# Another order of the work inside steps 1 to 5 of a fused attention and expert kernel

## The chip, the cores and the metric

The kernel runs on one core of a Trainium2 chip. The metric is the device time of one execution in microseconds (us). Each engine of the core (TensorE, VectorE, ScalarE, GpSimd, SyncE, in the profile PE, DVE, ACT, POOL, SP) has its own program; an instruction waits on semaphores, and everything behind it on its engine waits with it.

## The reference

Input x has 8 sequences of 256 tokens of width 256, and a context of the same shape. The layer adds an attention and then a mixture of experts:

```
x = x + attention(layernorm(x), ctx, ctx)          # 16 heads of 16, keys j < i only (and j = 0 for i = 0)
    scores = (q Wq)(k Wk)^T / 4 ; probs = softmax ; out = (probs (ctx Wv + bv)) Wo + bo
x = x + experts(layernorm(x))                      # 8 experts, 2 per token, at most 512 rows each
    top_k(softmax(x wg), 2) -> relu(x w1 + b1) w2 + b2, weighted by the gates
```

## The kernel before, in words

The function `attention` (line 45) handles the 8 sequences in a software pipeline of steps s = -2 to 8, written out by hand for every engine as a function `step(s)`; `experts` (line 1344) follows and is not changed. In a step s three sequences are at work: sequence s + 2 is normalised and projected to queries and keys; of sequence s + 1 the largest score of each row is found (the "maxima"), and its values are projected; of sequence s the scores, exponentials, masks and products with the values are made; and sequence s - 1 gets its output projection, second norm and router. Steps 1 to 5 contain all of these parts. Steps 0, 6, 7 and 8 have orders of their own.

Products in 32 bits are made from a high part (rounded by ScalarE) and a low part (the difference, from VectorE or GpSimd), in three matmuls: `project` and `project_turned` (lines 1113 and 1102) make 12 matmuls of 256 columns each. For the scores, queries and keys are cut in three bf16 parts h, m and l; SyncE copies each part to rows of a stacked tile, six transfers for queries and six for keys (`stack`, line 252), and one matmul over 126 or 128 rows then gives the score.

On TensorE `a_scores` (line 986) makes the maxima's scores in 12 units of two or four heads, in two PSUM banks in turn, so that a unit waits until VectorE has reduced the one two before it (`maxima`, line 718). Unit 0 also waits for all stacking transfers of the step before (lines 991 and 992). `split_maxima` (line 770), `turn_maxima` (line 1091) and ScalarE's `copy_maxima` (line 574) put the negative maxima into two more rows of the stacked queries by a transfer, for which `b_scores` of the next step waits (line 1009). `b_scores` (line 1006) makes the scores of a group of four heads in three banks (there is one such buffer, so the next group waits for the exponentials), `exp` (line 504) on ScalarE the exponentials, `mask` (line 390) on GpSimd the mask in three instructions, and `values` (line 1023) on TensorE the product with the values, line 1035 and 1036. ScalarE's `values` (line 513) copies two groups out. `turn_values` (line 1040) transposes them, `normalise` (line 727) divides by the sums, `turn_attention`, `outputs`, `turn_x2` and `router` follow on TensorE (lines 1081, 1147, 1085, 1164), with `round_attention`, `normalise_x2` and `copy_x2` on ScalarE (lines 519, 547, 552), `add_output`, `logits` and `top_two` on VectorE (lines 746, 765, 705).

Two PSUM banks, `bank[0]` and `bank[1]` (line 67), are shared by all of the small products. bank[0] takes the projected values, the second turned values, the transposed x, the keys and the router's result; bank[1] the first turned values, the transposed attention, the output projection, the queries, the transposed x2 and the turned maxima. So the order of these on TensorE sets which copies each must wait for.

The norm of x is made in parts: `next_stats` (VectorE, line 754), `norm_powers` (GpSimd, line 378) and `norm_x` (ScalarE, line 498), the last three sequences ahead of step s. `add_value_bias` (VectorE, line 735) waits for the values' projection, and the second `turn_values` waits for it (line 1047). `prefetch` (line 474) loads 1 MB of expert weights from ScalarE's queue.

## Time and profile before

| | us |
|---|---|
| median of 3 runs | 436.12 |
| lowest and highest of them | 433.43, 436.37 |
| profiled execution, its time | 436.96 |
| its span, first to last instruction | 435.2 |
| granted TensorE clock, mean over the span | 0.94 |
| busy in the span: PE, PEld, DVE, ACT, POOL | 372.6, 315.6, 291.4, 189.1, 213.5 |

The profile is one execution. Times in rows are us from the span's start. A row of a timeline has the start, the length (ns elsewhere), the engine, the line in the code, the operation with its output and inputs, how many instructions are merged (x4), and in brackets how long the engine idled before and what released it. PE are matmuls and PEld the weight loads, which overlap them. The end of a matmul contains the time in which its result drains, so a run of matmuls is best read from start to start. A row of busy time by stretch has the stretch and its length, then the busy time of PE, PEld, DVE, ACT and POOL with their counts of instructions, the granted TensorE clock (1.00 is 2.4 GHz), and the DMA engines' share and GB/s. Names of tiles stand without their numbers; tiles that share memory may stand under the name of another, such as w_hi and w_lo for the stacked queries and keys.

### The profile page before, as it was taken

The numbers are of one execution on the slowest core, as the hardware profiler recorded it, in microseconds if no ns is written. First come the engines' busy times: TensorE is split into PE (matmuls) and PEld (weight loads), VectorE is DVE, ScalarE is ACT, GpSimd is POOL, SyncE is SP. The second block draws the span as 40 slices with busy tenths as digits, with TensorE's granted clock in tenths as the row PEclk, the third lists the DMA queues.
The fourth block names the chain that finished last, engine by engine and source line by source line (L and its number), as shares of the span: only waits on it lengthen the run. The fifth ranks groups of instructions, "written<-read, shape, count | busy, mean of one in ns | idle before, by whom it ended". The sixth has DMA issues, their size and how long they took to land. (4 is left out here: it accounts for less than half of the span.)

```text
span 435.2 us, 8185 instructions
## 1 busy us (share of the span) xinstructions
PE 372.6 (86%) x3030; PEld 315.6 (73%) x3030; DVE 291.4 (67%) x627; ACT 189.1 (43%) x258; POOL 213.5 (49%) x305
## 2 busy tenths in 40 slices
PE   3686899999999997877453999999999999999991
PEld 3555676767776776665341899999999998989891
DVE  6576776776767666763781467786777778677840
ACT  4423555565646453664210535354353626262310
POOL 7659867574848372423226303526180817250532
PEclk9989999999999999986655899999999999999998
DMA  8983716060605164132223603728090918230223
GB/s 205 247 231 82 208 32 189 27 196 26 193 5 138 60 182 123 50 101 78 81 50 81 259 0 107 199 75 229 12 274 21 269 28 244 60 51 9 30 32 36
DMA packets 38315, 49.15 MB, mean 113 GB/s; under 512 B 7138, under 2 KB 34180, under 8 KB 37252
## 3 DMA queue, kind: packets, MB, share of 16 engines
q1 hardware_dynamic: 29636, 34.93, 27.7%
q0 software_dynamic: 6144, 8.33, 10.2%
q10 hardware_dynamic: 2496, 5.38, 3.9%
q8 instruction: 24, 0.39, 0.4%
q14 instruction: 15, 0.12, 0.1%
HBM read 27.60 MB, written 8.41 MB: 83 GB/s over the span
## 5 line engine op out<-in xcount | busy, mean ns | idle before, releaser
L1490 POOL DMA_INDIRECT out_dram<-Y,scatter_idx x32 | 51.3, 1603 | 106.5 <-DVE Y L1646 91.0
L1533 ACT ACTIVATE hr<-ps,b_sb 128x512 f32<-128x512 f32 x64 | 43.2, 686 | 99.5 <-PE ps L1690 57.5
L724 DVE TENSOR_REDUCE nm<-ps 128x2 f32<-128x512 f32 (+1 forms) x96 | 61.5, 681 | 17.4 <-PE ps L1003 17.2
L1700 PE MATMUL ps<-w_hi,h_hi 128*128 128x256 f32 x224 | 63.2, 282 | 0.0
L1700 PE MATMUL ps<-w_lo,h_hi 128*128 128x256 f32 x224 | 62.9, 281 | 0.0
L1700 PE MATMUL ps<-w_hi,h_lo 128*128 128x256 f32 x224 | 62.8, 280 | 0.0
L511 ACT ACTIVATE PT<-ps 128x1536 f32<-128x1536 f32 x32 | 46.5, 1452 | 22.7 <-PE ps L1019 21.7
L1621 DVE CAST h_hi<-hr 128x512 fp32r<-128x512 f32 x60 | 27.2, 454 | 39.2 <-ACT hr L1533 36.2
L1690 PE MATMUL ps<-XT_hi,w_hi 128*128 128x512 f32 x128 | 51.3, 401 | 1.5 <-DVE XT_lo L1604 1.5
L1690 PE MATMUL ps<-XT_hi,w_lo 128*128 128x512 f32 x128 | 51.2, 400 | 0.0
L1690 PE MATMUL ps<-XT_lo,w_hi 128*128 128x512 f32 x128 | 51.1, 400 | 0.0
L1700 PEld LDWEIGHTS ps<-w_hi,h_hi 128*128 128x128 f32 x224 | 42.2, 188 | 1.6
L1700 PEld LDWEIGHTS ps<-w_hi,h_lo 128*128 128x128 f32 x224 | 42.2, 188 | 1.5
L1623 DVE TENSOR_TENSOR h_lo<-hr,h_hi 128x512 fp32r<-128x512 f32 x60 | 41.7, 695 | 2.1
L1700 PEld LDWEIGHTS ps<-w_lo,h_hi 128*128 128x128 f32 x224 | 42.2, 188 | 0.0
L1477 POOL DMA_INDIRECT Xg<-xn_rows,gather_idx x32 | 32.5, 1014 | 12.5 <-issue 9.4
L1003 PE MATMUL ps<-mask,identb 128*128 128x256 bf16 (+1 forms) x96 | 30.0, 313 | 0.0
L1690 PEld LDWEIGHTS ps<-XT_hi,w_hi 128*128 128x128 f32 x128 | 24.6, 192 | 5.6 <-issue 1.9
L1690 PEld LDWEIGHTS ps<-XT_lo,w_hi 128*128 128x128 f32 x128 | 24.6, 192 | 5.5
L1690 PEld LDWEIGHTS ps<-XT_hi,w_lo 128*128 128x128 f32 x128 | 24.7, 193 | 3.9
L1035 PE MATMUL ps<-PT,V 128*32 128x256 f32 x256 | 22.0, 406 | 3.9 <-POOL PT L396 3.9
L394 POOL TENSOR_SCALAR_AFFINE_SELECT PT<-PT 128x4 f32<-128x4 f32 x32 | 6.5, 204 | 36.7 <-ACT PT L511 36.5
(234 smaller groups left out, 888.2 us busy)
## 6 DMA issues: line engine op xcount, KB each, us to landing
raw<-in_L_ffn_w_dram SPq DMA_DIRECT2D x12, 1024.0 KB
raw<-in_L_ffn_w_dram ACTq DMA_DIRECT2D x4, 1024.0 KB
c_sb<-in_ctx_dram SPq DMA_DIRECT2D x8, 256.0 KB, 4.3
xn_rows<-x2n SPq DMA_DIRECT2D x8, 256.0 KB, 3.0
out_dram<-x_all SPq DMA_DIRECT2D x8, 256.0 KB, 2.8
x_all<-in_x_dram SPq DMA_DIRECT2D x1, 1280.0 KB, 6.5
w_lo<-k_h SPq DMA_DIRECT2D x9, 128.0 KB, 3.5
w_hi<-q_h SPq DMA_DIRECT2D x9, 128.0 KB, 2.5
```

Of the source, the lines that this page charges most:

```text
L394: pool.affine_select(p0[:, :, 0:1], p0[:, :, 0:1], [[0, HPG], [0, 1]], ALU.is_ge, 0.0, base=0, channel_multiplier=-1)
L511: act.activation(PT[g % 2][:, :], prob_score, ACT.Exp, scale=float(HD) ** -0.5).then_inc(exp_done, 1)
L724: dve.tensor_reduce(nm[:, tile, h:h + count], max_bank[u % 2].rearrange("p (h j) -> p h j", h=count), AX_X, ALU.max, negate=True).then_inc ...
L1003: pe.matmul(diag, identb[:, :], mask1[:, :, :] if tile else mask0[:, :, :], start=False, stop=True, skip_group_check=True).then_inc(a_done, 1)
L1035: pe.matmul(out, V[s % 2][:, 0, h, :], PT[g % 2][:, hh * S:(hh + 1) * S], start=True, stop=False)
L1477: pool.indirect_dma_start(Xg[q][:, j, :], None, xn_rows[:, :], bass.IndirectOffsetOnAxis(ap=gather_idx[:, ST * e + j:ST * e + j + 1], axis ...
L1490: pool.indirect_dma_start(out_rows[:, :], bass.IndirectOffsetOnAxis(ap=scatter_idx[:, ST * e + j:ST * e + j + 1], axis=0), Y[q][:, j, :], ...
L1533: act.activation(hr[c % 2][:, :], h_bank[c % 4], ACT.Relu, bias=b1_sb[q][:, c:c + 1]).then_inc(hr_ready, 1)
L1621: dve.tensor_copy(h_hi_of(e, c), hr[c % 2][:, :]).then_inc(hh_ready, 1)
L1623: dve.tensor_tensor(h_lo_of(e, c), hr[c % 2][:, :], h_hi_of(e, c).bitcast(F32), ALU.subtract).then_inc(hl_ready, 1)
L1690: last = pe.matmul(h_bank[c % 4], w[q][:, k, c, :], a[q][:, k, :], start=(n == 1), stop=(n == 6))
L1700: last = pe.matmul(y_bank[j // 2][:, (j % 2) * D:(j % 2 + 1) * D], a[c % 4][:, j * P:(j + 1) * P], w[q][:, c, :], start=(c == 0 and n == 0 ...
```

## The change

Steps 1 to 5 get an order of their own on each engine.

- TensorE: maxima unit 0 stands between the two turned values; units are issued singly or in pairs through `unit_scores`. Keys are projected ahead of scores 2, and before queries. The output projection follows scores 1. The router and the turned maxima stand between values 2 and values 3, the maxima no longer wait for the router's copy but for the copy of x2. The next values' projection waits for the router's copy.
- VectorE: the top two of the router of the step before and the statistics of sequence s + 3 stand first, ahead of the value bias; the router's result is copied at the end of the step (`copy_logits`).
- ScalarE: `norm_x` of sequence s + 2 stands first in step s (before: that of s + 3 late in step s). `copy_maxima` and the last copy of values stand at the head of the next step, maxima first; exp 0 is ahead of rounding attention and x. The weights' load of step 5 comes last in it.
- GpSimd: powers of the next norm and the bias first, then the context; keys and queries are split on either side of mask 2.
- SyncE: stacks keys before queries, except in step 0.

```diff
--- before.py
+++ after.py
@@ -283,7 +283,7 @@
                 if proj_part(s):
                     if s + 2 >= BUFS:
                         sp.wait_ge(b_done, GROUPS * s)
-                    for row in (stack_keys, stack_queries) if s < 0 else (stack_queries, stack_keys):
+                    for row in (stack_queries, stack_keys) if s == 0 else (stack_keys, stack_queries):
                         row(s, to)
                 if out_part(s):
                     sp.wait_ge(x2n_ready, 2 * s)
@@ -419,6 +419,19 @@
                     mask(0, 2)
                     mask(0, 3)
                     norm_powers(3)
+                    return
+                if 0 < s < B - 2:
+                    if s + 3 < B:
+                        norm_powers(s + 3)
+                    add_bias(s + 2)
+                    split_context(s)
+                    mask(s, 0)
+                    mask(s, 1)
+                    powers(s - 1, ln2_stats, mv2, ve2, rs2, ln2_pow)
+                    split_keys(s)
+                    mask(s, 2)
+                    split_queries(s)
+                    mask(s, 3)
                     return
                 if proj_part(s):
                     split_context(s)
@@ -606,6 +619,27 @@
                     if score_part(s):
                         values(s, 1)
                     prefetch(s - (B - 2) + 2)
+                elif 0 < s < B:
+                    norm_x(s + 2)
+                    if s > 1:
+                        copy_maxima(s - 1)
+                        values(s - 1, 1)
+                    round_context(s)
+                    exp(s, 0)
+                    round_attention(s)
+                    round_x(s)
+                    exp(s, 1)
+                    round_keys(s)
+                    exp(s, 2)
+                    round_queries(s)
+                    normalise_x2(s)
+                    values(s, 0)
+                    exp(s, 3)
+                    copy_x2(s)
+                    if s == B - 3:
+                        copy_maxima(s)
+                        values(s, 1)
+                        prefetch(1)
                 else:
                     if proj_part(s) and s > 0:
                         round_context(s)
@@ -639,16 +673,12 @@
                     if score_part(s):
                         values(s, 0)
                         exp(s, 3)
-                    if 0 < s and s + 3 < B:
-                        norm_x(s + 3)
                     if s == 0:
                         copy_maxima(s)
                     if score_part(s):
                         values(s, 1)
                     if max_part(s) and s > 0:
                         copy_maxima(s)
-                    if s == 0:
-                        norm_x(3)
 
             round_weights(1)
             round_context(-2)
@@ -716,7 +746,10 @@
                     dve.tensor_copy(expert_all[:, k, bass.ds(2 * n, 2)], idx8[:, :, k]).then_inc(top_used, 1)
 
             def maxima(s, pair):
-                for u in (2 * pair, 2 * pair + 1):
+                unit_maxima(s, 2 * pair, 2 * pair + 2)
+
+            def unit_maxima(s, lo, hi):
+                for u in range(lo, hi):
                     dve.wait_ge(a_done, UNITS * (s + 1) + u + 1)
                     if u == 0 and not first(s, 0):
                         dve.wait_ge(nm_ready, 2 * (s + 1))
@@ -762,9 +795,12 @@
                     dve.wait_ge(xn_ready, 2 * (s + 2))
                 norm_stats(x_all[:, bass.ds(2 * (s + 3), 2), :], st1[(s + 3) % 2], mv1[(s + 3) % 2], ln1_stats, s + 3)
 
-            def logits(s):
+            def copy_logits(s):
                 dve.wait_ge(rt_done, s)
                 dve.tensor_copy(lg[:, :, :], bank[0][:, 0:2 * EXPERTS].rearrange("p (t e) -> p t e", t=2)).then_inc(lg_ready, 1)
+
+            def logits(s):
+                copy_logits(s)
                 top_two(s - 1)
 
             def split_maxima(s):
@@ -907,6 +943,29 @@
                     early_slots(1, 0)
                     early_slots(1, 1)
                     logits(s)
+                elif 0 < s < B:
+                    if s > 1:
+                        top_two(s - 2)
+                    if s + 3 < B:
+                        next_stats(s)
+                    add_value_bias(s)
+                    normalise(s, 0)
+                    unit_maxima(s, 0, 1)
+                    normalise(s, 1)
+                    unit_maxima(s, 1, 3)
+                    split_attention(s)
+                    split_x(s)
+                    unit_maxima(s, 3, 4)
+                    add_output(s)
+                    unit_maxima(s, 4, 5)
+                    split_keys(s)
+                    unit_maxima(s, 5, 8)
+                    split_queries(s)
+                    unit_maxima(s, 8, 12)
+                    split_maxima(s)
+                    copy_logits(s)
+                    if s == B - 3:
+                        top_two(s - 1)
                 elif s == 0:
                     maxima(s, 0)
                     maxima(s, 1)
@@ -985,8 +1044,11 @@
         def _(pe):
             def a_scores(s, pair):
 
+                unit_scores(s, 2 * pair, 2 * pair + 2)
+
+            def unit_scores(s, lo, hi):
                 Q, K = Qs[(s + 1) % BUFS], Ks[(s + 1) % BUFS]
-                for u in (2 * pair, 2 * pair + 1):
+                for u in range(lo, hi):
                     if u == 0:
                         pe.wait_ge(q_stacked, 96 * (s + 2))
                         pe.wait_ge(k_stacked, 96 * (s + 2))
@@ -1045,7 +1107,7 @@
                         pe.wait_ge(nmT_ready, s + 1)
                 elif max_part(s):
                     pe.wait_ge(v_ready, s + 2)
-                elif not score_part(s):
+                else:
                     pe.wait_ge(lg_ready, s - 1)
                 for g in range(GROUPS):
                     last = pe.transpose(bank[1 - t][:, g * P:(g + 1) * P], OT[:, g, t * P:(t + 1) * P], ident[:, :])
@@ -1091,7 +1153,7 @@
             def turn_maxima(s):
                 pe.wait_ge(nm_ready, 2 * (s + 2))
                 if out_part(s):
-                    pe.wait_ge(lg_ready, s)
+                    pe.wait_ge(x2T_ready, s)
                 else:
                     pe.wait_ge(k_rest_ready, s + 3)
                 for t in range(2):
@@ -1133,6 +1195,8 @@
 
             def keys(s):
                 pe.wait_ge(cT_lo_ready, s + 3)
+                if s > 0:
+                    pe.wait_ge(xT_lo_ready, s + 3)
                 if first(s, -1):
                     pe.wait_ge(w_lo_ready, 1)
                 project_turned(key_bank(s), 1, cT_hi, cT_lo, k_done)
@@ -1142,6 +1206,8 @@
                     pe.wait_ge(w_lo_ready, 3)
                 if s == 0:
                     pe.wait_ge(q_rest_ready, 1)
+                if s > 1:
+                    pe.wait_ge(lg_ready, s - 1)
                 project(values_bank(s), 2, cT_hi, cT_lo, v_done)
 
             def outputs(s):
@@ -1272,6 +1338,33 @@
                         turn_maxima(s)
                     if score_part(s):
                         values(s, 3)
+                elif 0 < s < B:
+                    project_values(s)
+                    turn_values(s, 0)
+                    unit_scores(s, 0, 1)
+                    turn_values(s, 1)
+                    b_scores(s, 0)
+                    unit_scores(s, 1, 3)
+                    turn_attention(s)
+                    turn_x(s)
+                    unit_scores(s, 3, 5)
+                    b_scores(s, 1)
+                    outputs(s)
+                    values(s, 0)
+                    keys(s)
+                    b_scores(s, 2)
+                    unit_scores(s, 5, 7)
+                    queries(s)
+                    unit_scores(s, 7, 8)
+                    values(s, 1)
+                    unit_scores(s, 8, 10)
+                    b_scores(s, 3)
+                    turn_x2(s)
+                    unit_scores(s, 10, 12)
+                    values(s, 2)
+                    router(s)
+                    turn_maxima(s)
+                    values(s, 3)
                 else:
                     if max_part(s):
                         project_values(s)
```

## Rows read from the trace of the kernel before

**Rows 1.** Busy time by stretch: step 2, and steps 7 and 8 to the experts' first matmul.

```profile
97.50:120.00 22.50, 20.86 (x220) 16.70 (x219) 16.08 (x42) 12.73 (x18) 14.30 (x26) 1.00 0.38 107
...
186.00:239.00 53.00, 29.65 (x247) 22.01 (x248) 28.65 (x84) 16.15 (x23) 19.66 (x32) 0.63 0.28 80
```

**Rows 2.** TensorE's waits in steps 1 to 5: total us, times, longest.

```profile
PE ps L1035 <- POOL PT L396: 3.5, 6, 0.6
PE ps L1051 <- DVE V L741: 2.1, 6, 0.3
PE ps L1120 <- DVE aT_lo L694: 1.6, 5, 0.3
```

**Rows 3.** TensorE's timeline of step 2: start, length, line, operation, idle before.

```profile
97.48 0.38 PE L1120 MATMUL ps<-w_hi,cT_hi 128*128 128x256 f32 x1
...
99.00 0.60 PE L1051 MATMUL ps<-ident,OT 128*128 128x128 f32 x4
...
113.39 0.95 PE L1174 MATMUL ps<-wg_sb,x2T 128*128 128x8 f32 x8
114.28 0.66 PE L1035 MATMUL ps<-PT,V 128*32 128x256 f32 x8
...
115.09 0.61 PE L1016 MATMUL ps<-w_hi,w_lo 128*128 128x256 bf16 x4
...
115.76 0.39 PE L1000 MATMUL ps<-Ks,Qs 126*128 126x128 bf16 x4
...
116.20 0.38 PE L1000 MATMUL ps<-Ks,Qs 126*128 126x256 bf16 x2
...
117.44 0.39 PE L1000 MATMUL ps<-Ks,Qs 126*128 126x256 bf16 x2
...
117.78 0.39 PE L1000 MATMUL ps<-Ks,Qs 126*128 126x128 bf16 x4
...
119.02 0.66 PE L1035 MATMUL ps<-PT,V 128*32 128x256 f32 x8 [0.64 <-POOL PT L396]
...
119.98 0.39 PE L1120 MATMUL ps<-w_hi,cT_hi 128*128 128x256 f32 x1
```

**Rows 4.** VectorE's timeline of step 2: split maxima before it, bias, statistics, reductions.

```profile
97.02 0.19 DVE L777 TENSOR_TENSOR nm_s<-nm,nm_s 128x32 bf16<-128x32 f32 x1
99.20 0.69 DVE L741 TENSOR_TENSOR V<-ps,bv_bc 128x512 f32<-128x512 f32 x1 [1.99 <-PE ps L1120]
...
109.30 0.74 DVE L681 BATCH_NORM_STATS2 st<-x_all 128x6 f32<-128x256 f32 x2
110.15 0.25 DVE L684 BATCH_NORM_AGGREGATE mv<-st 128x2 f32<-128x6 f32 x2
...
111.71 2.57 DVE L724 TENSOR_REDUCE nm<-ps 128x2 f32<-128x512 f32 x4
```

**Rows 5.** ScalarE's timeline of step 2: the copy of x2 and exp 3.

```profile
111.70 0.60 ACT L489 ACTIVATE x2T<-ps 128x512 f32<-128x512 f32 x1 [0.63 <-PE ps L1058]
...
115.96 1.45 ACT L511 ACTIVATE PT<-ps 128x1536 f32<-128x1536 f32 x1
```

**Rows 6.** GpSimd's timeline of step 2: the last instruction of mask 3.

```profile
118.32 0.65 POOL L396 TENSOR_SCALAR_AFFINE_SELECT PT<-PT 128x512 f32<-128x512 f32 x1
```

**Rows 7.** SP's timeline, steps 2 and 3: three transfers of a high part.

```profile
113.16 1.85 SPq L257 DMA_DIRECT2D w_hi<-k_h  x3
...
135.35 3.25 SPq L257 DMA_DIRECT2D w_lo<-k_h  x3
```

**Rows 8.** Transfers of steps 1 to 5: count, KB each, median us from issue to landing.

```profile
Qs<-q_l SPq DMA_DIRECT2D x2, 128.0 KB, 5.1
...
w_lo<-q_l SPq DMA_DIRECT2D x1, 128.0 KB, 2.6
```

**Rows 9.** VectorE's timeline at the end of step 0: the split maxima.

```profile
50.57 0.53 DVE L777 TENSOR_TENSOR nm_s<-nm,nm_s 128x32 bf16<-128x32 f32 x1
```

**Rows 10.** TensorE's timeline in step 6: its first scores.

```profile
168.82 0.61 PE L1016 MATMUL ps<-w_hi,w_lo 128*128 128x256 bf16 x4 [0.81 <-DMA w_hi<-nmT]
```

## The prediction

> **What bounds the kernel now.** I read four views in this order: busy time by stage, TensorE's waits, TensorE's timeline of one step, and then the other engines beside it.
>
> The stages show where the change acts. Steps 1 to 5 take 22.5 us each (step 2 stands in the rows; the four others repeat it to 0.1 us), 112.5 us together. TensorE is busy 20.9 us of such a step, VectorE 16.1, GpSimd 14.3, ScalarE 12.7, and the granted clock is 1.00, the 2.4 GHz level [rows 1]. TensorE therefore leads these steps, and only its idle time can be gained: no matmul is removed. The experts behind them are not touched.
>
> TensorE's waits name three idle places that come back in nearly every step: 0.6 us for the mask of the fourth group of probabilities, 0.35 us for the biased values, 0.3 us for the low half of the attention output [rows 2]. The timeline shows them in step 2, which runs from 97.48 to 119.98 [rows 3]. A wait also empties the array (its pipeline has run dry when the wait ends), so I count differently: which start-to-start times does the array need for the work itself? From [rows 3]: a projection 1.52 (97.48 to 99.00), router 0.89, values of a group 0.81, scores of a group 0.67, a four-head maxima unit 0.44, a two-head unit 0.34, turned maxima and what ends before them 0.96 with the last values (119.02 to 119.98), so 0.2 alone. Four transposes I put at 0.45 (an estimate: x4 stand with 0.60 including the drain). The step has 4 projections (6.1), 5 sets of transposes (2.25), 4 scores (2.7), 4 values (3.2), 8 two-head and 4 four-head units (4.5), the router (0.9) and the turned maxima (0.2): 19.85 us. So 22.5 - 19.85 = 2.65 us of each step are gaps, 13.2 us in five steps. This is the most that an order can give there.
>
> **The change part by part.** I walk one new step; times are us after its first projection starts, durations those of before. VectorE takes the biased values 1.72 after the step's start for 0.69 us [rows 4]; exp starts 0.87 after its scores start (115.09 to 115.96), takes 1.45, and its mask ends 1.6 after the exp ends (117.41 to 118.97) [rows 3, 5, 6].
>
> *Start.* Values' projection 0 to 1.52, first turned values to 1.97, maxima unit 0 to 2.31. The second turned values need the bias, done at 2.41, and start at 2.47: the 0.5 us gap of before is 0.16, since unit 0 fills it. Then scores 0 (2.92 to 3.59) and units 1, 2 (to 4.37). VectorE does normalise, unit 0, normalise in about 2.0 us from 2.3, to 4.3, just before the attention's transposes (4.37 to 4.82); x's follow to 5.3, units 3, 4 to 5.98, scores 1 (exp 0 ended at 5.24) to 6.65. ScalarE now does exp 0 ahead of rounding attention and x, so the low half of the attention output is ready at about 6.5; the output projection needs it only at 6.65. That gap is gone, with 0.1 to spare.
>
> *Middle.* Outputs to 8.17, values 0 to 8.98, keys to 10.5, scores 2 to 11.17, units 5, 6 to 11.95, queries to 13.47, unit 7 to 13.8, values 1 to 14.6, units 8, 9 to 15.4, scores 3 to 16.07. Each maxima unit must wait until VectorE has reduced the one two before it. VectorE's reductions come each 0.64 us [rows 4]; in my walk units 4, 6, 9, 10 and 11 find theirs done 0.1 to 1 us earlier. No gap, little room. The next statistics (0.74 and 0.25 with a semaphore between, 1.1 us, [rows 4]) and the top two of the previous router (nine small instructions, an estimate of as much again) now stand at the head of the step, where VectorE idled 1.99 us for the projection [rows 4]. They end at about 1.65, bias due at 1.72: they cost nothing, and would cost what they are late.
>
> *End.* x2's transposes to 16.5, units 10, 11 to 17.3, values 2 to 18.1. Exp 3 runs 16.27 to 17.72, then the copy of x2 (0.60, [rows 5]) to 18.25: the router waits 0.15 us and runs to 19.15, turned maxima to 19.37. The mask of group 3 ends at 17.72 + 1.6 = 19.3, so the last values start at 19.37 with almost no wait, where they stood idle 0.64 us (0.8 with the drain). This is the largest gain: between the last scores and the last values lay 3.93 us, of which 2.8 were filled; now the chain exp and mask is covered by x2, two units, values 2, router and turned maxima. Values end at 20.1. The next projection waits for the router's copy (about 19.6): nothing.
>
> The sum is 19.85 + 0.16 + 0.15, so 20.15. Splitting the units makes two more switches between kinds of matmul; each such first matmul starts about 0.08 later than one in a run, so 0.15 more: 20.3. Five steps give 5 x (22.5 - 20.3) = 11.0 us.
>
> *Transfers.* This is the added risk. Unit 0 stood behind both sets of turned values, scores 0 and two sets of transposes and is now 2 us into the step, and it needs all twelve stacking transfers of the step before. Keys first: their high part is ready at 11.3, and SP issues three in 1.85, so one each 0.62 us [rows 7]. GpSimd's two parts of each take some 1.9 us (an estimate: one of its 512-element instructions takes 0.65, [rows 6], and the second part has two inputs, so I count three of them). With them the last key transfer is issued at 14.6; queries follow from 15.2, the last at 18.4, ready on GpSimd since 17.3. It lands 2.6 us later [rows 8] at 21.0, unit 0 of the next step is due at 20.3 + 1.97 = 22.3: 1.3 us to spare. Not counted.
>
> *Step 6.* Its first scores waited 0.81 us for the turned maxima's transfer [rows 10]. These maxima are now turned ahead of the last values, 0.8 us earlier, and copied ahead of the last output copy. Between 0 and 0.97 us are gained (its other waits stay); I take 0.2 to 0.5, say 0.3. The load of expert weights moves behind step 5's copies, and about 15 us lie before its use: nothing lost, and it no longer runs among the stacking transfers. GpSimd's reordering and SP's keys ahead of queries only serve this order and are priced in it.
>
> *A lock.* In step 0 the second half of the split maxima took 0.53 us beside GpSimd's mask [rows 9], against 0.19 at the end of step 1 [rows 4]; in the new steps it falls beside the mask of group 3. At 0.53 the maxima are ready at 19.1, before the router has ended: nothing. The Trainium skill, "SBUF — State Buffer", section "SBUF: two separate sides", says that VectorE with two SBUF inputs and GpSimd exclude each other for whole instructions. By it the split could stand behind the last mask instruction, 19.3 + 0.2 = 19.5, which would put 0.3 us on each step, 1.5 in all.
>
> **The sum.** The profiled execution took 436.96 us (span 435.2). 436.96 - 11.0 - 0.3 = 425.7. The median of the runs, 436.1, is 0.84 lower, so I forecast 424.9.
>
> **The rivals.**
>
> *The stacking comes late, and it gets slower.* Unit 0 stands ahead of everything but the projection and one set of transposes; while it waits, TensorE's queue stands, and with it the scores, exp and masks. For it: the first three issues have taken 3.25 instead of 1.85 us once [rows 7], and two last query transfers took a median of 5.1 us [rows 8]. Each us beyond 1.3 counts fully, five times. Both in every step (2.8 from keys' and queries' issues, 2.5 from the landing) would be 5.3 - 1.3 = 4.0 us per step against 2.2 gained: 424.9 + 20 = 445. It decides from 3.5 us of lateness. Against it: the 5.1 contains a landing beside the 1 MB load, which moves away, and 3.25 stood in one step of five. Slower: 0.05.
>
> *VectorE becomes the bound in part.* It is busy 16.1 us a step [rows 1], some 17 with its own semaphores, and 20.3 leave 3. It must now wait in its order for unit 7 and the router's end. If maxima come 1 us late once or twice, a step takes 21.3: 425.7 + 5 - 0.8 = 430. The small margins above speak for it; that I took its durations with their semaphores speaks against. 0.17.
>
> *Nothing moves.* The gaps return elsewhere in the step: 22.2 to 22.5, so 433 to 436. That would want a loop through two steps that keeps the period; I find the longest one, scores 3, exp, mask, last values, projection, bias, below 20.2. 0.06.
>
> **How the numbers follow.** Forecast 0.72, its own range 421.5 to 428: below, every gap vanishes (13.2 + 0.97, 422 after rounding); above, 0.5 us more a step. With VectorE's case the range is 421 to 431. The clock adds its own uncertainty: it averages 0.63 between step 6 and the experts [rows 1], and where it returns may move, as the earlier runs spread by 3 us. About 1% can be told from no change: faster than 431.8 holds in the forecast and most of VectorE's case, 0.87; within 1% 0.08; slower 0.05.
>
> **What would show it.** Steps 1 to 5 about 20.3 us long; the wait of the last values for the mask near 0; the bias wait at 0.1 to 0.2; a short router wait for x2's copy; no wait of unit 0 for a transfer; statistics ahead of the bias; steps 6 onward as long as before. I am wrong if TensorE stands before unit 0, if maxima units wait for VectorE by more than 1 us in a step, or if the part behind step 5 grows.

## The result, and the profile after

The changed kernel takes 421.35 us (median of 3 runs, 419.91 to 422.76) against 436.12 us: the ratio is 0.9707 (95% interval [0.9666, 0.9747], as in all brackets behind a ratio). That is 14.8 us gained where 11.2 were forecast (424.9). It is inside the range of 421 to 431, at its lower edge, and just below the 421.5 at which the forecast's own range ended. The profiled execution took 422.76 us with a span of 421.0, so in the spans 14.2 us are gone. This section reads where they went; from here on "step n" starts with its first projection, as in the prediction.

Busy time by stretch of the changed kernel: step 3 and step 6 (columns: the stretch, its length, busy us and instructions of TensorE, its weight loads, VectorE, ScalarE, GpSimd; granted clock; share of the DMA engines; GB/s).

```profile
93.85:114.12 20.27, 19.87 (x219) 16.92 (x218) 16.45 (x44) 12.53 (x17) 14.26 (x26) 1.00 0.44 123
155.35:175.38 20.03, 17.06 (x192) 13.44 (x191) 14.67 (x40) 11.71 (x14) 7.06 (x16) 1.00 0.37 120
```

Step 3 holds TensorE busy for 19.87 of 20.27 us, where step 2 before held it for 20.86 of 22.50 [rows 1]. VectorE's and GpSimd's sums hardly move. TensorE's sum is 1.0 us smaller though no matmul was removed; the end of a matmul contains the time in which its result drains, so I read this as fewer stops behind which it shows (argued, not shown by a run). The five steps take 20.46, 20.27, 20.27, 20.27 and 20.96 us, before they took 22.44 to 22.51.

TensorE's waits in steps 1 to 5 of the changed kernel, 53.12 to 155.35 (us in total, times, longest).

```profile
PE ps L1078 <- DMA w_lo<-nmT: 0.7, 1, 0.7
PE ps L1062 <- issue: 0.3, 1, 0.3
```

These two stand where the five steps before had 6.5 us in three kinds of wait. ([rows 2] reaches into the steps on either side: from 52.53 to 164.93 the mask has 3.2 in 5 times and the bias 1.7 in 5.) The waits for the mask, the bias and the low half of the attention output are gone in all five steps. The wait of 0.3 is unit 0's in step 1. The 0.7 for the transfer of the turned maxima is in step 5, which is the one long step.

TensorE's timeline of step 3, changed kernel (start, length, engine, line, operation).

```profile
93.85 0.39 PE L1182 MATMUL ps<-w_hi,cT_hi 128*128 128x256 f32 x1
...
95.37 0.60 PE L1113 MATMUL ps<-ident,OT 128*128 128x128 f32 x4
96.05 0.39 PE L1062 MATMUL ps<-Ks,Qs 126*128 126x256 bf16 x2
...
96.39 0.60 PE L1113 MATMUL ps<-ident,OT 128*128 128x128 f32 x4
...
99.80 0.60 PE L1078 MATMUL ps<-w_hi,w_lo 128*128 128x256 bf16 x4
...
100.43 0.37 PE L1182 MATMUL ps<-w_hi,aT_hi 128*128 128x256 f32 x1
...
109.24 0.60 PE L1078 MATMUL ps<-w_hi,w_lo 128*128 128x256 bf16 x4
...
111.21 0.66 PE L1097 MATMUL ps<-PT,V 128*32 128x256 f32 x8
...
112.09 1.06 PE L1240 MATMUL ps<-wg_sb,x2T 128*128 128x8 f32 x8
113.20 0.29 PE L1160 MATMUL ps<-identb,nm_s 128*32 128x128 bf16 x2
113.32 0.65 PE L1097 MATMUL ps<-PT,V 128*32 128x256 f32 x8
...
114.12 0.38 PE L1182 MATMUL ps<-w_hi,cT_hi 128*128 128x256 f32 x1
```

Taken from 93.85, unit 0 starts at 2.20, the second turned values at 2.54, scores 1 at 5.95, the output projection at 6.58, scores 3 at 15.39, values 2 at 17.36, the router at 18.24, the turned maxima at 19.35, the last values at 19.47. The prediction's walk had 1.97, 2.47, 5.98, 6.65, 15.4, 17.3, 18.25, 19.15 and 19.37. No time of the walk is off by more than 0.25 us.

VectorE around the seam of steps 3 and 4, changed kernel: statistics and bias at the head, then the split maxima and the router's copy at the end.

```profile
94.09 0.74 DVE L711 BATCH_NORM_STATS2 st<-x_all 128x6 f32<-128x256 f32 x2
94.94 0.25 DVE L714 BATCH_NORM_AGGREGATE mv<-st 128x2 f32<-128x6 f32 x2
95.57 0.69 DVE L774 TENSOR_TENSOR V<-ps,bv_bc 128x512 f32<-128x512 f32 x1 [0.38 <-PE ps L1182]
...
112.19 0.34 DVE L811 CAST nm_s<-nm 128x32 bf16<-128x32 f32 x1
112.57 0.57 DVE L813 TENSOR_TENSOR nm_s<-nm,nm_s 128x32 bf16<-128x32 f32 x1
113.19 0.17 DVE L800 COPY lg<-ps 128x16 f32<-128x16 f32 x1
```

GpSimd's timeline beside it, the last instruction of mask 3.

```profile
112.46 0.65 POOL L396 TENSOR_SCALAR_AFFINE_SELECT PT<-PT 128x512 f32<-128x512 f32 x1
```

The idle time ahead of the bias fell from 1.99 [rows 4] to 0.38: the statistics fill it and still end in time. At the end the second half of the split took 0.57 us beside GpSimd's mask; it ended at 113.14, the mask at 113.11. The turned maxima and the last values follow at 113.20 and 113.32. So mask, maxima and router (112.09 + 1.06) end within 0.05 us of each other, and a further gain at one of them would find the two others there.

**The part behind step 5.** The profiled pair divides as follows (before less changed, from the starts of the same operations): steps up to 1, -0.6; steps 1 to 5, 10.2; step 6 to step 7's first turned values, 1.0 (21.08 to 20.03); from there to step 8's first turned values, 2.75 (18.94 to 16.19); to the experts' first matmul, 0.1; experts, 0.7. Together 14.2. TensorE's timeline shows the 2.75, first in the kernel before, then in the changed one.

```profile
186.01 1.97 PE L1051 MATMUL ps<-ident,OT 128*128 128x128 f32 x8 [1.16 <-ACT OT L517]
...
200.87 1.87 PE L1174 MATMUL ps<-wg_sb,x2T 128*128 128x8 f32 x8 [0.19 <-ACT x2T L489]
204.95 1.97 PE L1051 MATMUL ps<-ident,OT 128*128 128x128 f32 x8 [0.75 <-ACT OT L517]
```

```profile
175.38 1.09 PE L1113 MATMUL ps<-ident,OT 128*128 128x128 f32 x8 [1.16 <-ACT OT L530]
...
188.88 1.06 PE L1240 MATMUL ps<-wg_sb,x2T 128*128 128x8 f32 x8 [0.84 <-ACT x2T L502]
191.57 1.97 PE L1113 MATMUL ps<-ident,OT 128*128 128x128 f32 x8 [0.74 <-ACT OT L530]
```

The instructions are the same, but before they met the 1.2 GHz level twice, at the step's start (1.97 against 1.09) and at its router (1.87 against 1.06); the changed kernel met it only from 190.9 on. The prediction had put 0.3 us on all that lies behind step 5.

### The profile page after: what moved, and what is told of

It is laid out like the page before. It is cut to its first block and busy times, and to the rows that moved or that the text cites. A ratio compares the mean times of both kernels' runs of the same rounds, so it can differ in the third digit from the quotient of the medians.

```text
span 421.0 us, 8170 instructions
## 1 busy us (share of the span) xinstructions
PE 364.5 (87%) x3010; PEld 314.1 (75%) x3030; DVE 293.9 (70%) x627; ACT 188.2 (45%) x258; POOL 215.9 (51%) x305
## 5 line engine op out<-in xcount | busy, mean ns | idle before, releaser
L757 DVE TENSOR_REDUCE nm<-ps 128x2 f32<-128x512 f32 (+1 forms) x96 | 62.4, 682 | 18.7 <-PE ps L1065 11.2
L1570 POOL DMA_INDIRECT Xg<-xn_rows,gather_idx x32 | 34.9, 1090 | 12.3 <-issue 9.3
L1065 PE MATMUL ps<-mask,identb 128*128 128x256 bf16 (+1 forms) x76 | 22.5, 296 | 0.0
L1097 PE MATMUL ps<-PT,V 128*32 128x256 f32 x256 | 21.1, 390 | 1.5 <-POOL PT L396 0.7
```

The lines of the kernel that those rows point to most:

```text
L757: dve.tensor_reduce(nm[:, tile, h:h + count], max_bank[u % 2].rearrange("p (h j) -> p h j", h=count), AX_X, ALU.max, negate=True).then_inc ...
L1065: pe.matmul(diag, identb[:, :], mask1[:, :, :] if tile else mask0[:, :, :], start=False, stop=True, skip_group_check=True).then_inc(a_done, 1)
L1097: pe.matmul(out, V[s % 2][:, 0, h, :], PT[g % 2][:, hh * S:(hh + 1) * S], start=True, stop=False)
L1570: pool.indirect_dma_start(Xg[q][:, j, :], None, xn_rows[:, :], bass.IndirectOffsetOnAxis(ap=gather_idx[:, ST * e + j:ST * e + j + 1], axis ...
```

## The experiments

Two questions were open. Which parts of the new order carry the 2.2 us of a step: one of them, or only all together? And is what was gained behind step 5 the order's or only the clock's?

**1. Both kernels again.** No edit.

> The kernel before once more. Both theories: steps 1 to 5 take 112.4 us. Theory A, chance: the clock's fall, which in the first profile stood over step 7's first turned values, can stand elsewhere here, and the part behind step 6's start (270.3 us) comes out between 267 and 272. Theory B, the order sets it: the fall stands at the same place, 270.3 within 0.5. The ratio to the runs beside it is 1.000 within 0.004 by both.

> The changed kernel once more, to see which part of its gain is fixed and which moves. Both theories: steps 1 to 5 again take 102.2 us together (20.3 each, step 5 up to 0.7 more), step 6 starts about 155.4. Theory A, chance: where the granted clock falls in steps 7 and 8 and where it returns in the experts moves from execution to execution by up to about 3 us, so the part behind step 6's start (265.6 us in the first profile) comes out anywhere between 264 and 269, and the time between 419.5 and 425. Theory B, the denser steps themselves keep the clock up into step 7: the clock is again at its high level over step 7's first turned values (1.09 us for 8 transposes, not 1.97), and the part behind step 6's start is 265.6 within 0.5.

Measured: before again 435.34 us, ratio 0.9988 [0.9942, 1.0034], steps of 22.47 to 22.61. Changed again 423.69 (420.78 to 427.02), ratio 0.9765 [0.9674, 0.9857], steps 20.97, 20.27, 20.35, 20.26, 20.72. TensorE's timeline of before again has step 7 like this:

```profile
186.82 1.09 PE L1051 MATMUL ps<-ident,OT 128*128 128x128 f32 x8 [1.16 <-ACT OT L517]
...
200.35 1.88 PE L1174 MATMUL ps<-wg_sb,x2T 128*128 128x8 f32 x8 [0.23 <-ACT x2T L489]
204.43 1.97 PE L1051 MATMUL ps<-ident,OT 128*128 128x128 f32 x8 [0.75 <-ACT OT L517]
```

The same kernel, the same work: 17.61 us instead of 18.94, with the fall at the step's start gone. Changed again took 17.34, having met a fall there. What the five steps gain repeats to 0.2 us; what step 7 gains does not (2.75, then 0.3). Theory B, as it was put, has failed: the fall did not keep its place in either kernel.

**2. The end of the step alone, on the order of before.** Router and turned maxima ahead of the last values, ScalarE's and VectorE's order to suit; and then the whole end, with x2's transposes late, as in the changed kernel.

```diff
# tail_alone, TensorE; scores 5 is the pair of units 10 and 11
-                    if out_part(s):
-                        router(s)
                     if score_part(s):
                         values(s, 1)
                         b_scores(s, 3)
...
                         a_scores(s, 5)
+                    if out_part(s):
+                        router(s)
+                    if out_part(s) and max_part(s):
+                        turn_maxima(s)
                     if score_part(s):
                         values(s, 3)
-                    if max_part(s):
+                    if max_part(s) and not out_part(s):
                         turn_maxima(s)
# tail_whole, in addition, the end as it then reads
+                        a_scores(s, 4)
+                    if score_part(s):
+                        b_scores(s, 3)
+                    if out_part(s):
+                        turn_x2(s)
+                    if max_part(s):
+                        a_scores(s, 5)
+                    if score_part(s):
+                        values(s, 2)
```

> The kernel before with only the tail changed: router and turned maxima ahead of the last values, the router's copy behind the split maxima, the maxima copied first. My theory: the 0.8 us gap before the last values is filled, and the turned maxima's transfer starts earlier, 0.9 to 1.1 us less a step, step length 21.4 to 21.6, 4.5 to 5.5 us in all and up to 0.9 in step 6: time 0.985 to 0.990 of the kernel before. Rival, that one part of this order gives nothing while the others bound the step: 0.995 to 1.000.

> The kernel before with the whole tail of the changed one in its steps: units 8 and 9, scores 3, x2's transposes, units 10 and 11, values 2, router, turned maxima, last values; the copy of x2 behind exp 3. Theory, after the run with the router alone moved (where the last reductions took the place of the mask): the gap closes only if the maxima's reductions too are covered, here by values 2 and router behind unit 11; step length 21.6 to 21.9, so 3 to 4.5 us over five steps, with 0.1 to 0.2 us left before the last values. Rival, the tail is worth nothing as long as the first half has its gaps: 22.3 to 22.5, and a new wait of 0.6 us appears in the tail.

Measured: 433.35 us (0.9942 [0.9899, 0.9986]), steps of 22.37 to 22.42; and 434.14 (0.9989 [0.9947, 1.0032]), steps of 22.45 to 22.51. The mask wait did go in both. TensorE's waits of steps 1 to 5 show what took its place, first for the end alone, then for the whole end. (The wait for the low half of the attention output stayed too, 1.6 in both.)

```profile
PE ps L1098 <- DVE nm_s L777: 2.9, 5, 0.6
PE ps L1051 <- DVE V L741: 1.6, 5, 0.3
```

```profile
PE ps L1000 <- DVE nm L724: 2.8, 5, 0.6
PE ps L1051 <- DVE V L741: 1.6, 5, 0.3
```

Five times 0.6 us for VectorE: for the split maxima in the one, for the reduction that frees a unit's bank in the other. VectorE's reductions were late by about as much as the mask, and showed once the wait for the mask no longer hid them. My theory fell here, and with it the reading of [rows 2] in which the mask wait's 0.64 us are there for whoever covers the mask.

**3. The end and the middle together.** To the whole end were added the next statistics at the head of VectorE's step, and units 4 and 5 with their reductions ahead of the keys' projection. GpSimd's order stayed.

```diff
# VectorE
+                    if s + 3 < B:
+                        next_stats(s)
                     if max_part(s):
                         add_value_bias(s)
...
                         split_queries(s)
-                    if s + 3 < B:
-                        next_stats(s)
+                    if max_part(s):
+                        maxima(s, 2)
                     if proj_part(s):
                         split_keys(s)
                     if max_part(s):
-                        maxima(s, 2)
                         maxima(s, 3)
```

> The kernel before with the changed tail and also room for VectorE in the middle: the next statistics stand first in the step, and units 4 and 5 and their reductions ahead of the keys. Theory, after the run with the tail alone, in which the wait for the mask vanished and unit 6 waited 0.56 us for a reduction instead: the gap in the tail and the gap in the middle are one budget of VectorE, and both close together; step length 21.5 to 21.9 (22.5 less about 0.7 to 0.9), 3 to 4.5 us in all, no wait of a unit over 0.3. Rival, the period is kept by the start of the step (bias, low half of attention): 22.3 to 22.5 whatever is done behind.

Measured: 434.13 us (0.9971 [0.9934, 1.0008]), steps 22.35, 23.61, 23.53, 23.50, 21.42. The waits for reductions went, and the mask wait came back. The timelines of ScalarE (first row) and GpSimd at the seam of steps 1 and 2, and below them TensorE's:

```profile
70.79 1.45 ACT L511 ACTIVATE PT<-ps 128x1536 f32<-128x1536 f32 x1 [0.97 <-PE ps L1020]
...
71.71 0.23 POOL L366 TENSOR_SCALAR ve<-mv 128x2 f32<-128x2 f32 x1
...
73.26 0.20 POOL L371 TENSOR_TENSOR rs<-ve,rs 128x2 f32<-128x2 f32 x1
73.40 0.21 POOL L394 TENSOR_SCALAR_AFFINE_SELECT PT<-PT 128x4 f32<-128x4 f32 x1
...
74.18 0.65 POOL L396 TENSOR_SCALAR_AFFINE_SELECT PT<-PT 128x512 f32<-128x512 f32 x1
```

```profile
74.89 0.66 PE L1036 MATMUL ps<-PT,V 128*32 128x256 f32 x8 [0.83 <-POOL PT L396]
...
76.33 0.41 PE L1121 MATMUL ps<-w_lo,cT_hi 128*128 128x256 f32 x1
...
78.46 1.64 PE L1052 MATMUL ps<-ident,OT 128*128 128x128 f32 x8
```

Exp 3 had ended at 72.24 (70.79 + 1.45), but GpSimd's order still had the powers of the next statistics (71.71 to 73.46) between mask 2 and mask 3, and the mask started at 73.40. So the new place of these powers, at the head of GpSimd's step, is a part of the change in its own right, which the prediction had not priced apart. Then, in steps 2 to 4, the granted clock fell to the 1.2 GHz level just behind this idle stretch: projection matmuls took 0.41 instead of 0.28 and two sets of transposes 1.64. Steps 2 to 4 are 1.2 us longer each than step 1, which had the same mask wait and no fall. Step 5 has no further sequence to norm, so no powers stand ahead of its mask 3; it had neither mask wait nor fall and took 21.42, where the kernel before took 22.47. So about 1.1 us of the 2.2 is there by then, read from one step of one profile. This run bears out neither theory whole.

**4. One part of the new order undone.** Each on the changed kernel: the router and the turned maxima behind the last values; unit 0 behind both sets of turned values and scores 0 (with its reduction); exp 0 behind the roundings of attention and x.

```diff
# router_last
                     values(s, 2)
+                    values(s, 3)
                     router(s)
                     turn_maxima(s)
-                    values(s, 3)
# unit0_behind
                     turn_values(s, 0)
-                    unit_scores(s, 0, 1)
                     turn_values(s, 1)
                     b_scores(s, 0)
-                    unit_scores(s, 1, 3)
+                    unit_scores(s, 0, 3)
# exp0_behind
-                    exp(s, 0)
                     round_attention(s)
                     round_x(s)
+                    exp(s, 0)
                     exp(s, 1)
```

> The changed kernel with router and turned maxima behind the last values in steps 1 to 5. My theory, that these two cover the chain exp, mask: the last values now wait for the mask 1.1 to 1.3 us, router and turned maxima (1.1) come after them, and the next projection waits 0.2 for the router's copy, so each step is 1.1 to 1.4 us longer: 5.5 to 7 us, 427 to 428.5. Rival, that the gain of these steps comes from their first half (bias, low half of attention) and the tail's order is hidden: under 2 us, below 423.5.

> The changed kernel with unit 0 behind both turned values, as before. Theory: the wait for the biased values is back, 0.35 us idle and 0.5 with the drain instead of 0.1: 0.3 to 0.4 us a step, 20.6 to 20.7, 1.5 to 2 us in all. Rival 1, VectorE has no room: units 1 and 2 are reduced 0.6 us later, and further waits of units follow, 20.9 or more. Rival 2: hidden by later room, 20.3.

> The changed kernel with exp 0 behind the rounding of attention and x on ScalarE. Theory: exp 0 starts 6.2 instead of 3.8 us into the step and ends 7.6, scores 1 start 1.6 us later, and with them everything behind: step length 21.6 to 22.0, 7 to 8.5 us more. Rival, the scores' buffer has room in this order: under 0.5 us a step.

| kernel | median us | ratio to before | steps 1 to 5 | over changed (102.2) |
|---|---|---|---|---|
| router last | 430.41 | 0.9884 [0.978, 0.9987] | 109.8 | 7.6 |
| unit 0 behind | 428.12 | 0.9875 [0.9794, 0.9955] | 106.9 | 4.7 |
| exp 0 behind | 428.49 | 0.986 [0.9779, 0.994] | 110.4 | 8.2 |

The long waits of each in TensorE's queue over steps 1 to 5, in the order of the table:

```profile
PE ps L1097 <- POOL PT L396: 5.4, 5, 1.1
```

```profile
PE ps L1061 <- DVE nm L757: 2.3, 5, 0.5
PE ps L1112 <- DVE V L774: 1.6, 5, 0.3
```

```profile
PE ps L1078 <- ACT PT L524: 7.1, 5, 1.4
```

Router last has one fall of the granted clock in it, in step 4 (mean 0.93, 22.68 us where its others take 21.59 to 21.87), so some 0.8 of its 7.6 us are the clock's; the other two have none. Each part taken out brings its own wait in every step: the mask (1.07 us in each), the bias and the reductions, or exp 0 itself, for which scores 1 now stood 1.4 us. Unit 0 is the telling one. The bias wait of 0.35 returns and costs what the prediction gave it, but 0.5 comes on top because VectorE, later by one reduction, holds a unit up further on: the rival that VectorE has no room was right where it was tested. Against them stands experiment 2: the end alone, put on the old order, is worth 0.1 us a step or nothing. (The start alone was not tried on it.) I read the 2.2 us as those of three chains (ScalarE's exps, GpSimd's masks, VectorE's reductions) that come due together; the waits that replace each other in experiments 2 to 4 show it for these parts, while the keys' new place and the halves of GpSimd's split were not undone by themselves.

**5. The transfers.** Queries stacked ahead of keys on the changed kernel, so that the last keys leave late; and two 64 KB transfers more on SP's queue between the keys' and the queries' in each of the five steps.

```diff
# queries_first
-                    for row in (stack_queries, stack_keys) if s == 0 else (stack_keys, stack_queries):
+                    for row in (stack_keys, stack_queries) if s < 0 else (stack_queries, stack_keys):
# extra_2
                         if row is stack_queries and 0 < s:
                             for _ in range(2):
                                 sp.dma_start(extra_rows[2 * (s - 1) + _], ident[:, :]).then_inc(extra_done, 16)
```

> The changed kernel with SyncE stacking queries ahead of keys in steps 1 to 5. Theory, that unit 0 stands 1.2 us behind the last landing: the last key transfer is now issued about 21.0 us into the step and lands 2.5 us later, unit 0 waits for a transfer in steps 2 to 5 (and the units of step 6 do not), step length 21.2 to 21.7, 4 to 6 us more in all. Rival, that the landing has more room than I read: no wait of unit 0, 20.3 us a step.

> The changed kernel with two more transfers of 64 KB issued by SyncE between the keys' and the queries' stacking in steps 1 to 5. In the changed kernel's trace the last query transfer lands 0.8, 0.05, 1.4 and 0.8 us before unit 0 of steps 2 to 5. The extra ones make it 1.2 to 1.3 us later. Theory, that this room is all there is: unit 0 waits 0.4, 1.2, 0 and 0.4, and the steps are longer by as much, 1.5 to 2.5 us in all. Rival, my forecast's room of 1.3: no wait.

Measured for queries first: 438.92 us (437.9 to 439.91), ratio 1.0118 [1.0036, 1.02], steps 20.82, 22.48, 24.10, 21.62, 21.79. For two more transfers: 426.76 (422.4 to 428.13), 0.9795 [0.9763, 0.9828], steps 20.18, 20.98, 20.79, 20.27, 21.31. TensorE's waits of steps 1 to 5 for queries first and, below, for the two transfers:

```profile
PE ps L1062 <- issue: 8.5, 5, 2.4
```

```profile
PE ps L1068 <- DMA w_hi<-q_l: 1.9, 2, 1.1
PE ps L1068 <- DMA Qs<-q_l: 0.7, 1, 0.7
```

SP's timeline of queries first at the start of step 3 (93.16):

```profile
91.36 1.83 SPq L257 DMA_DIRECT2D Ks<-k_h  x3
93.24 1.52 SPq L257 DMA_DIRECT2D Ks<-k_m  x2
94.81 0.61 SPq L257 DMA_DIRECT2D Ks<-k_l  x1
```

The last key transfer is issued 1.65 us into the step whose unit 0 needs it at 2.2. Keys are projected first, so behind the queries they wait for no reason, and all the rest of TensorE's queue waits with unit 0. The five steps take 110.8 us, 8.6 more than changed (one fall of the clock, in step 3, is in that), and the expectation of 4 to 6 was too small. It also said that step 6 would be spared, and there the longest wait stood:

```profile
169.38 0.58 PE L1062 MATMUL ps<-Ks,Qs 126*128 126x256 bf16 x2 [4.98 <-issue]
```

The last keys of step 5 were issued at 162.26, behind the 1 MB load (161.27), and took 7.0 us to land. Step 6 took 26.15 us instead of 20.03, again with a fall of the clock. So this is the rival of the late stacking: in the five steps it takes most of the gain away (110.8, before 112.4), and only step 6 makes the kernel slower than before, by 1.2% in the medians. The one line of the diff in SP's loop is what keeps it away. Two more transfers make three waits, 2.6 us together, of which 1.3 remain in the five steps (103.5 against 102.2): a delay of about 1.2 us (two issues of 0.61) is on the edge. In the changed kernel the last query transfer of steps 1 to 4 lands at 74.72, 96.0, 114.69 and 135.62, and unit 0 of the next step starts at 75.5, 96.05, 116.1 and 136.45. The forecast 1.3 us to spare were 0.8, 0.05, 1.4 and 0.8. The 0.05 is no margin at all but a short wait: the weight load of unit 0 in step 3 (PEld) stood idle for this transfer.

```profile
PEld ps L1062 <- DMA Qs<-q_l: 0.3, 1, 0.3
```

**6. The load of expert weights at its old place**, in the middle of step 5's work on ScalarE, all else as changed.

```diff
                     normalise_x2(s)
+                    if s == B - 3:
+                        prefetch(1)
                     values(s, 0)
                     exp(s, 3)
                     copy_x2(s)
                     if s == B - 3:
                         copy_maxima(s)
                         values(s, 1)
-                        prefetch(1)
```

> The changed kernel with step 5's 1 MB load back at its earlier place, ahead of the third copy of values. Theory: the load's packets stand among step 5's stacking transfers and delay the turned maxima's transfer, for which step 6's first scores wait again, 0.5 to 1 us, while step 5 itself stays at 20.7 to 21.0: 0.5 to 1.5 us in all. Rival 1: step 6's units wait for the stacked queries as well, more than 2 us. Rival 2: nothing, since the transfer of the maxima starts earlier in this order.

Measured: 426.13 us (423.75 to 430.41), ratio 0.9764 [0.9719, 0.9809]. The profiled execution took 430.41 us, so I compare step 6 alone. It starts at 155.42, in the changed kernel at 155.35. TensorE's timeline of its first scores, here and in the changed kernel:

```profile
161.40 0.65 PE L1079 MATMUL ps<-w_hi,w_lo 128*128 128x256 bf16 x4 [2.89 <-DMA w_hi<-nmT]
```

```profile
158.31 0.60 PE L1078 MATMUL ps<-w_hi,w_lo 128*128 128x256 bf16 x4
```

The 1 MB load was issued at 148.82, among the stacking transfers and 6.5 us ahead of the turned maxima's 16 KB on ScalarE's own queue. The transfers of q's high part took a median of 6.7 us to land (2.8 in the changed kernel), and the maxima's landed 6 us after its issue at 155.28. Step 6 then took 24.08 us instead of 20.03, with one fall of the clock in it. That is more than the 0.5 to 1 us expected. In the changed kernel the two stand the other way round: maxima issued at 155.21, load at 155.96. So in this execution the load's old place costs 2.9 us by its wait. Whether it costs the kernel as much in the others isn't shown: the medians point the same way (426.1 against 421.4 and 423.7), but the executions overlap, and the ratio is that of changed again (0.9765). The 7.0 us landing beside the same load in queries first points to the same mechanism. In the kernel before, the load also ran ahead of the maxima (157.32 and 165.87), 8.5 us ahead, and 0.81 us were waited [rows 10].

**7. Work for TensorE in its gaps from step 8 to the experts.** 37 more matmuls into a bank that nobody reads, the output unchanged. The first 15 are shown; the other 22 stand ahead of the experts' first matmuls.

```diff
+            def fill(n):
+                for _ in range(n):
+                    pe.matmul(ps[:, 3, :], identb[:, :], mask0[:, :, :].rearrange("p h j -> p (h j)"), start=True, stop=True)
...
+                    fill(2)
                     turn_values(s, 0)
                     turn_values(s, 1)
                     early_counts()
...
+                    fill(3)
                     last_outputs()
+                    fill(10)
```

> The changed kernel with 37 matmuls of 512 columns into a free bank where TensorE waits between step 8 and the first expert, each group shorter than the wait even at the low clock (10 in the 4.7 us before x2's transposes, 10 in the 4.8 us before the gathered rows). Theory, that the low clock there (1.2 GHz for 27 to 37 us) comes from TensorE's idle time and costs through the transposes, the last output projection and the first expert matmuls: the granted clock is high for most of this part, the part from step 6's start to the end is 2 to 5 us shorter, 417 to 420. Rival, the fill is too thin to hold the clock: no change or up to 1 us longer.

Measured: 422.11 us (420.68 to 423.52), ratio 0.9701 [0.9666, 0.9735]. Busy time by stretch, step 6 to the experts' first matmul, here and in changed again:

```profile
152.58:223.04 70.46, 51.86 (x477) 35.00 (x474) 43.13 (x124) 27.85 (x37) 26.63 (x48) 0.88 0.32 95
```

```profile
152.45:222.60 70.15, 43.40 (x440) 32.90 (x437) 43.14 (x124) 27.84 (x37) 26.46 (x47) 0.79 0.31 92
```

The granted clock rose from 0.79 to 0.88 and the stretch stayed at 70 us, where 2 to 5 us less for all behind step 6's start were expected. The last output projection ran at 0.28 a matmul instead of 0.41, and the time went back to waits for VectorE and GpSimd, which lead there. No kernel of this study is clearly faster than the changed one.

## Why the prediction was right, point by point

*The step: right.* Forecast 20.3, measured 20.27 in three of five, and each place of the walk within 0.25 us. The stream of 19.85 us, counted by start-to-start times, the small bias gap (second turned values at 2.54, forecast 2.47) and the router's start held. The router took 0.2 more than counted (1.11 to the turned maxima), these 0.1 less. The 0.15 for two more switches I can't find at its own place: unit 0's start 0.2 later than in the walk is the wait for the last query transfer in step 3, and in step 2, without it, unit 0 and the second turned values start at 1.96 and 2.47, as in the walk. *Steps 1 and 5* are 0.2 and 0.7 longer than the sum had them: a wait of unit 0 (0.3, and 0.9 in changed again, whose step 1 took 20.97), and the turned maxima's transfer, whose 16 KB I had priced in step 6 only. So the five steps gained 10.2 instead of 11.0. This term failed by size: the walk was made for a middle step and multiplied by five.

*The start, the middle, the end.* That unit 0 fills the bias gap is shown by experiment 4, at 0.9 us a step if undone. Undoing exp 0's place costs 1.6, but not by the wait that the prediction spoke of: the wait for the attention's low half stays away there, and scores 1 stand for exp 0 instead. So exp 0 ahead serves scores 1; that the low half's wait is gone may be due to the output projection's new place behind scores 1, which no run undid. "No gap, little room" is right to the letter: one reduction later and a unit waits 0.5. "This is the largest gain", said of the end, is right in one direction only: undone it costs about 1.35 a step (7.6 less the fall's 0.8, over five), alone it brings 0.1 or nothing, which the prediction did not say and which its own list of 0.1 us margins would have told.

*Transfers: right in kind, small in room.* 1.3 us forecast, 0.05 to 1.4 measured, though the last issue came at 18.42 into step 3 as forecast (18.4), and at 18.6, 18.8 and 19.1 into steps 1, 2 and 4. The landing took 2.4 us in step 3, and 3.6 in the step before (issued at 92.35, landed at 96.0). The same two stores follow it on the queue in both, so why it took longer stays open. "No wait of unit 0 for a transfer" therefore missed in one step, by 0.2 us of its start, which the bias gap took up. The chance of 0.05 for this rival stood on a margin that one step had used up.

*The lock.* Forecast 0.53 for the second half, ready at 19.1, at no cost. Measured 0.57, and the cast before it also went from 0.18 to 0.34: ready at 19.29. The router ended there too, so about 0.1 us a step was paid (from the router's start to the turned maxima 1.11, and 0.99 in router last, where the split had long been done), in place of nothing or of 0.3. The Trainium skill's rule ("SBUF — State Buffer", section "SBUF: two separate sides") has the two engines exclude each other for whole instructions. The trace agrees that VectorE is held up beside GpSimd (0.57 against 0.19), but the split ended with the mask's last instruction (113.14 and 113.11) and not 0.2 us behind it.

*Step 6: right in sign, small in size.* 0.3 forecast within bounds of 0 and 0.97, measured 0.93 at its first scores. The load's move, taken as "nothing lost", was taken too lightly: in the one profile with the load put back, step 6's first scores stood 2.9 us.

*Behind step 5: the term that failed.* The sum carried the clock as a mere uncertainty of some 3 us. Of the 3 us beyond the forecast in the profiled pair, 2.75 lie in step 7, where no instruction differs. The lower end of the range was meant for the case that every gap vanishes; that the result came out there is luck, since the five steps gained 0.8 less than forecast. Fourteen profiles of this study give step 7's length.

| step 7, us | kernels |
|---|---|
| 16.17 to 16.19 (no fall ahead of its last us) | changed, clock filled, end and middle, router last, unit 0 behind, exp 0 behind, two transfers |
| 17.34 to 17.61 (one) | changed again; before again, end alone |
| 18.93 to 19.07 (both) | before; whole end; queries first, load early |

Both orders have members at each level, so the order doesn't fix it. It may still shift the odds: of the nine profiles with the new order six have no fall, and the two with both had a long transfer wait in step 6, while of the five with the old order only one has none. Fourteen profiles don't settle that, and why the fall takes one place or another stays open. The repeated pair of profiles is 16.0 us apart (435.0 and 419.0), of which 3.6 stand ahead of step 1, 10.0 in steps 1 to 5, 0.8 in step 6, 0.3 in step 7, 1.0 behind it and 0.3 in the experts. The share that is sure to be the order's is therefore read from steps 1 to 6: 10.2 + 1.0 = 11.2 in the first pair, 10.0 + 0.8 = 10.8 in the second, against 11.3 forecast. What the median had beyond that was no part of the predicted mechanism; by ratios the forecast, 424.9 / 436.1 = 0.974, lies between the two measurements, 0.9707 and 0.9765.

## What to carry to other kernels

When one wait ends a step, list which other engines' chains come due within the same microsecond: the wait's length is not its worth, and covering it alone can bring nothing. Walk the new step with start-to-start times of the old one and write the margin of each handover; where several are below 0.5 us, expect a part to be worth more undone than done alone, as the end was here (about 1.35 and 0.1 us), and take the queues that issue transfers into the walk. Compare kernels by the stretches that the edit touches, in two profiles each, before any of the rest is put down to it.

## What the runs showed of the hardware

The granted clock fell at different places in runs of the same work, and one such place is worth 1.2 to 1.4 us here (16.19, 17.6 and 18.94 us for one step). The stretch ahead of step 1 varied as much: step 1 started at 53.12 and 49.88 in two profiles of the changed kernel, at 52.53 and 53.47 in those of the kernel before. Filling TensorE's gaps held the clock up (0.79 to 0.88) and gained no time. In the third experiment it fell right behind three of four TensorE waits of 0.83 us and cost 1.2 us each time, with router last behind one of five waits of 1.07, and in the kernel before behind none of five of 0.64; no run tells what made the difference. A small subtraction of VectorE took 0.57 us beside a GpSimd mask and 0.19 alone, a cast 0.34 and 0.18. And transfers behind a 1 MB load land late: a 16 KB one issued 6.5 us behind it on the same queue took 6 us and held TensorE up for 2.9, and one of 128 KB issued 1 us behind it on another queue took 7.0 and held it up for 5.0.
